# A two-layer kernel with routed experts: one address read per block, zero rows written by GpSimd, second weights' low parts made by TensorE and ScalarE

## What is computed

```python
x = x + _L0_attn_ref(_layernorm(x), W1, b1, W2, b2, W3, b3, A)   # softplus mixing
x = x + _L0_ffn_ref(_layernorm(x), Wr, Wg, Wu, Wd)               # 9 experts, top 2
x = x + _L1_attn_ref(_layernorm(x), Wk, Wq, Wv, Wu, ...)         # 16 heads, causal
x = x + _L1_ffn_ref(_layernorm(x), centroids, ...)               # 64 experts, top 8
```

## Time and profile before

| | us |
|---|---|
| median of 3 runs | 1093.57 (1092.96 to 1095.56) |
| the profiled execution, its own time | 1094.27 |
| its span in the profile | 1092.5 |
| PE busy in the span | 954.4 (87%) |
| DVE, ACT, POOL busy | 833.8, 698.2, 469.8 |
| share of the chain: PE, DVE, SyncE's queue | 59%, 12%, 10% |

### The profile page before, as it was taken

How to read it: one execution, slowest core, us unless ns; L and a number is a source line. 1 busy time by engine, 2 the same in 40 slices (tenths; PEclk the granted TensorE clock), 3 DMA queues, 4 the chain that set the end, 5 groups by cost and what they waited for, 6 DMA issues and landing times.

```text
span 1092.5 us, 20812 instructions
## 1 busy us (share of the span) xinstructions
PE 954.4 (87%) x6055; PEld 758.4 (69%) x6088; DVE 833.8 (76%) x1938; ACT 698.2 (64%) x1387; POOL 469.8 (43%) x540
## 2 busy tenths in 40 slices
PE   3573698988936999999999998999999999999998
PEld 2452687878825677767777666877777777777786
DVE  6988465666647788888888766888888878797865
ACT  3560344444424877777778765777777777777876
POOL 3578760000046565556555330444444443444343
PEclk8655799999966999999999998999999999999999
DMA  8991321111120101101101001929375655657483
GB/s 255 411 391 68 100 61 55 53 52 52 54 70 18 30 23 26 35 21 28 33 21 30 11 1 37 222 71 202 96 175 119 152 138 133 150 120 173 104 193 81
DMA packets 70164, 111.00 MB, mean 102 GB/s; under 512 B 16783, under 2 KB 55858, under 8 KB 65970
## 3 DMA queue, kind: packets, MB, share of 16 engines
q1 hardware_dynamic: 65376, 101.31, 35.4%
q0 software_dynamic: 4096, 8.40, 2.6%
q10 hardware_dynamic: 594, 0.09, 0.0%
HBM read 70.90 MB, written 38.86 MB: 100 GB/s over the span
## 4 chain that ended last, share of the span: by engine, by line
PE 59%; DVE 12%; SPq 10%; issue 7%; DMA 5%; ACT 4%; POOL 1%; DVEq 0%; POOLq 0%; ACTq 0%
SPq L536 4%; PE ps L2322 4%; PE ps L2340 4%; PE ps L2324 4%; PE ps L2323 4%; PE ps L2342 4%; PE ps L2341 4%; PE ps L2126 4%; DMA cwB<-cwd 3%; PE ps L2189 3%; PE ps L2150 3%; PE ps L2144 3%; PE ps L2172 3%; SPq L546 2%; SPq L539 2%
## 5 line engine op out<-in xcount | busy, mean ns | idle before, releaser
L880 POOL TENSOR_TENSOR hl<-h,hh 128x512 fp32r<-128x512 f32 x128 | 167.7, 1310 | 257.5 <-ACT hh L1158 257.5
L1158 ACT ACTIVATE hh<-h 128x512 fp32r<-128x512 f32 (+1 forms) x264 | 165.4, 626 | 33.1 <-DVE h L1889 30.3
L1889 DVE TENSOR_TENSOR h<-ps,cwB 128x512 f32<-128x512 f32 x192 | 130.0, 683 | 44.8 <-ACT ps L1147 32.6
L1789 DVE TENSOR_REDUCE nm<-ps 128x4 f32<-128x512 f32 (+1 forms) x128 | 116.4, 952 | 36.7 <-PE ps L2172 34.6
L778 POOL DMA_INDIRECT yg<-ys,gps x64 | 62.7, 980 | 177.5 <-issue 167.0
L1147 ACT ACTIVATE ps<-ps 128x512 f32<-128x512 f32 x192 | 111.7, 582 | 35.4 <-PE ps L2324 34.2
L2322 PE MATMUL ps<-xh,wh 128*128 128x512 f32 x256 | 103.8, 405 | 0.5 <-ACT h L1145 0.5
L1896 DVE TENSOR_TENSOR hl<-h,hh 128x512 fp32r<-128x512 f32 (+1 forms) x136 | 96.3, 708 | 10.2 <-ACT hh L1158 8.9
L2340 PE MATMUL ps<-hh,wh 128*128 128x512 f32 x256 | 102.9, 402 | 0.6 <-POOL hl L880 0.6
L2324 PE MATMUL ps<-xh,wl 128*128 128x512 f32 x256 | 100.3, 392 | 0.0
L2323 PE MATMUL ps<-xl,wh 128*128 128x512 f32 x256 | 100.3, 392 | 0.0
(11 more groups left out here) (356 smaller groups left out, 2677.9 us busy)
## 6 DMA issues: line engine op xcount, KB each, us to landing
cwB<-cwd SPq DMA_DIRECT2D x32, 1536.0 KB, 14.9
ys<-zfill SPq DMA_DIRECT2D x13, 1536.0 KB, 21.4
cwd<-cwS SPq DMA_DIRECT2D x64, 96.0 KB
xb<-xs SPq DMA_DIRECT2D x72, 64.0 KB, 1.8
ys<-yb SPq DMA_DIRECT2D x72, 64.0 KB, 1.6
x_res<-in_L_attn_x_dram SPq DMA_DIRECT2D x4, 512.0 KB, 6.6
wst<-in_L_ffn_W_up_dram SPq DMA_DIRECT2D x32, 64.0 KB, 2.1
wst<-in_L_ffn_W_down_dram SPq DMA_DIRECT2D x32, 64.0 KB, 1.9
```

The source lines that it names most:

```text
L880: pool.tensor_tensor(hl4[:, slot(u), :], h4[:, slot(u), :], hh4[:, slot(u), :].bitcast(F32), op=ALU.subtract).then_inc(u_hlp, 1)
L1158: act.activation(hh4[r, slot(u), :], h4[r, slot(u), :], ACT.Copy).then_inc(u_hh, 1)
L1789: ins = dve.tensor_reduce(nm[:, u, 4 * g:4 * g + 4], o, axis=AX.X, op=ALU.max, negate=True)
L1889: dve.tensor_tensor(h4[:, slot(u), :], first, second, op=ALU.mult).then_inc(u_h, 1)
```

## The change

- SyncE's loops are written out. A block's row is read once (`rows_at`), for the load, and the register is kept for the store.
- The nine zero stores become nine indirect scatters on GpSimd after the 64 others; `tail` now holds a row per partition. The load of block 24 still waits for them.
- Pieces 6 to 8: ScalarE makes the high parts, first in the new `HIGH_ORDER`. For the low part TensorE adds identity times `std` and negated identity times the high part in PSUM, an expert at a time (`w2_diffs`), and ScalarE copies it out (`w2_lows`): four experts in turn 4, four in turn 5, the ninth behind. The first list's bank is 2 in place of 1. `w_low(0)` moves from turn 3 to turn 4.
- Constants that only the lists need are made behind GpSimd's `zfill`, not ahead of the first wait on `consts`.
- The fills count on `c_in`, waited for ahead of the first loads; the wait for the row positions (`gp_r`) and weights stands behind block 28's load, only before the q, k, v weights are loaded.

```diff
+    FILLS = NFILL // 3 + 1
...
+        HIGH_ORDER = (6, 7, 8, 0, 1, 2, 3, 4, 5)
...
-            def rows_of(blocks, b):
-                return ds(sp_.value_load(blocks[0:1, ds(b, 1)], min_val=0, max_val=SPARE + E1 * REG - P), P)
-            def load_block(b, u, blocks):
-                sp_.dma_start(xb[:, u, :], xs[rows_of(blocks, b), :]).then_inc(xb_in[u], 16)
+                              zfill[:, :].unsqueeze(1).broadcast_to([P, 3, FILL * D])).then_inc(c_in, 16)
+            rows_at = {}
+            def load_block(b):
+                blocks = blk_a if b < NFULL else blk_b
+                rows_at[b] = sp_.value_load(blocks[0:1, b:b + 1], min_val=0, max_val=SPARE + E1 * REG - P)
+                sp_.dma_start(xb[:, b % 4, :], xs[ds(rows_at[b], P), :]).then_inc(xb_in[b % 4], 16)
             for u in range(4):
                 sp_.sem_inc(ys_out[u], 16)
-            def store_block(b, u, blocks):
+            def store_block(b):
                 sp_.wait_ge(yb_r, b + 1)
-                sp_.dma_start(ys[rows_of(blocks, b), :], yb[:, u, :]).then_inc(ys_out[u], 16)
-            def next_block(b, u, blocks):
-                sp_.wait_ge(xT_r, b + 1)
-                load_block(b + 4, u, blocks)
-                if not isinstance(b, int) or b >= 2:
-                    store_block(b - 2, (u - 2) % 4, blocks)
+                sp_.dma_start(ys[ds(rows_at.pop(b), P), :], yb[:, b % 4, :]).then_inc(ys_out[b % 4], 16)
             sp_.wait_ge(lists, 1)
             for s in range(2):
                 sp_.wait_ge(scat[s], SCATTERED)
+            sp_.wait_ge(c_in, 16 * FILLS)
             for b in range(4):
-                load_block(b, b, blk_a)
-            sp_.wait_ge(tails_in, 16 * (NFILL // 3 + 1))
-            for b in range(4):
-                next_block(b, b, blk_a)
-            sp_.wait_ge(tails, 1)
-            for e in range(E1):
-                first_row = sp_.value_load(tail[0:1, e:e + 1], min_val=0, max_val=SPARE + E1 * REG - P)
-                sp_.dma_start(xs[ds(first_row, P), :], zrow[:, :]).then_inc(tails_in, 16)
-            with sp_.Fori(1, NFULL // 4 - 1) as it:
-                for u in range(4):
-                    next_block(it * 4 + u, u, blk_a)
-            sp_.wait_ge(lists, 2)
-            sp_.wait_ge(tails_in, 16 * (NFILL // 3 + 1 + E1))
-            for s in range(2):
-                sp_.wait_ge(scat[s], SCATTERED * (NR // 2))
-            sp_.wait_ge(gp_r, 1)
-            sp_.wait_ge(w_lo, 9)
-            for u in range(4):
-                next_block(NFULL - 4 + u, u, blk_b)
-            for j, w in enumerate((WqT, WkT, WvT)):
-                sp_.dma_start(wqkv[:, j * D:(j + 1) * D], w).then_inc(c_in, 16)
-            for j, w in enumerate((qln_w, kln_w, qln_b, kln_b)):
-                sp_.dma_start(ln8[:, j, :], w.rearrange("(a n) -> a n", a=1).broadcast_to([P, S])).then_inc(c_in, 16)
-            with sp_.Fori(NFULL // 4, NBLK // 4 - 1) as it:
-                for u in range(4):
-                    next_block(it * 4 + u, u, blk_b)
-            for b in range(NBLK - 6, NBLK):
-                store_block(b, b % 4, blk_b)
+                load_block(b)
+            for b in range(NBLK):
+                if b + 4 == NFULL:
+                    sp_.wait_ge(lists, 2)
+                    sp_.wait_ge(tails_in, 16 * E1)
+                    for s in range(2):
+                        sp_.wait_ge(scat[s], SCATTERED * (NR // 2))
+                if b + 4 < NBLK:
+                    sp_.wait_ge(xT_r, b + 1)
+                    load_block(b + 4)
+                if b >= 2:
+                    store_block(b - 2)
+                if b == NFULL:
+                    sp_.wait_ge(gp_r, 1)
+                    sp_.wait_ge(w_lo, 6)
+                    sp_.wait_ge(tc1, 2 * NR + E1)
+                    for j, w in enumerate((WqT, WkT, WvT)):
+                        sp_.dma_start(wqkv[:, j * D:(j + 1) * D], w).then_inc(c_in, 16)
+                    for j, w in enumerate((qln_w, kln_w, qln_b, kln_b)):
+                        sp_.dma_start(ln8[:, j, :], w.rearrange("(a n) -> a n", a=1).broadcast_to([P, S])).then_inc(c_in, 16)
+            for b in range(NBLK - 2, NBLK):
+                store_block(b)
...
-            own.done(pool.memset(lev_w[:, :, :], 0.0))
-            own.done(pool.memset(spare[:, :], 0.0))
-            own.done(pool.memset(lcnt[:, E1:E1 + 1], float(NFULL + 1)))
-            for dst, pattern, cm, b0 in ((rev9[:, :, :], [[0, RT], [-1, E1]], 0, E1), (half_off[:, :, :], [[0, 2], [-REG, E1]], 0, -SPARE),
-                                         (base[:, :], [[REG, E1]], 0, SPARE), (w99[:, :, :], [[1, E1], [-1, E1]], 0, 0),
-                                         (prow[:, :], [[0, E1]], 1, 0), (entry[:, :], [[1, NBLK]], 0, 1)):
+            for dst, pattern, cm, b0 in ((rev9[:, :, :], [[0, RT], [-1, E1]], 0, E1), (base[:, :], [[REG, E1]], 0, SPARE),
+                                         (prow[:, :], [[0, E1]], 1, 0)):
                 own.done(pool.iota(dst, pattern=pattern, base=b0, channel_multiplier=cm,
...
-            for piece in range(6, 9):
-                src, hi, lo, arrived, n = weight_piece(piece)
-                if piece == 6:
-                    pool.wait_ge(consts, 2)
-                    pool.wait_ge(arrived, 16 * n)
-                    apart(pool, pool_passed)
-                own.link(pool.tensor_copy(hi, src))
-                own.link(pool.tensor_tensor(lo, src, hi.bitcast(F32), op=ALU.subtract))
-                pool.sem_inc(w_lo, 1)
+            pool.wait_ge(consts, 2)
...
+            pool.wait_ge(tails, 1)
+            apart(pool, pool_passed)
+            for e in range(E1):
+                pool.indirect_dma_start(out=xs, out_offset=bass.IndirectOffsetOnAxis(ap=tail[:, e:e + 1], axis=0),
+                                        in_=zrow[:, :], in_offset=None).then_inc(tails_in, 16)
             pool.wait_ge(gp_r, 1)
-            pool.wait_ge(w_lo, 9)
-            pool.wait_ge(tails_in, 16 * (NFILL // 3 + 1 + E1))
+            pool.wait_ge(w_lo, 6)
+            pool.wait_ge(tc1, 2 * NR + E1)
+            pool.wait_ge(tails_in, 16 * E1)
...
+            act.activation(negi[:, :], ident[:, :], ACT.Copy, scale=-1.0)
...
+            def w2_lows(e0, e1):
+                for e in range(e0, e1):
+                    act.wait_ge(tr1, 2 * NR + e + 1)
+                    act.activation(wd2[:, e * JC:(e + 1) * JC, 1, :], bank[e % 2][:, 0:JC * D].rearrange("p (j d) -> p j d", d=D),
+                                   ACT.Copy).then_inc(tc1, 1)
...
+                if k >= NR:
+                    w2_lows(4 * (k - NR), 4 * (k - NR) + 2)
                 if two:
                     copy_T(xmT, 6, tc2, tr2, r, 0)
                     copy_T(xmT, 6, tc2, tr2, r, 1)
                 if mix:
                     softplus(1)
+                if k >= NR:
+                    w2_lows(4 * (k - NR) + 2, 4 * (k - NR) + 4)
...
-                    if k < NR:
-                        for piece in range(3 * (k - 2), 3 * (k - 1)):
+                    if k <= NR:
+                        for piece in HIGH_ORDER[3 * (k - 2):3 * (k - 1)]:
                             w_high(piece)
             rounds(act_round)
+            w2_lows(8, E1)
...
+                dve.wait_ge(consts, 3)
...
-                    dve.tensor_copy(tail[:, :], base[:, :]).then_inc(tails, 1)
+                    dve.tensor_tensor(tail[:, :], base[:, :], prow[:, :], op=ALU.add).then_inc(tails, 1)
...
-                if 3 <= k <= NR:
-                    w_low(k - 3)
+                if k == NR:
+                    w_low(0)
+                    w_low(1)
...
+            def w2_diffs(e0, e1):
+                for e in range(e0, e1):
+                    if e == 0:
+                        pe.wait_ge(w_hi, 3)
+                    if e >= 2:
+                        pe.wait_ge(tc1, 2 * NR + e - 1)
+                    o = bank[e % 2][:, 0:JC * D]
+                    pe.matmul(o, ident[:, :], std[:, e * JC * D:(e + 1) * JC * D], start=True, stop=False)
+                    pe.matmul(o.rearrange("p (j d) -> p j d", d=D), negi[:, :], wd2[:, e * JC:(e + 1) * JC, 0, :], start=False,
+                              stop=True).then_inc(tr1, 1)
...
+                if k >= NR:
+                    w2_diffs(4 * (k - NR), 4 * (k - NR) + 2)
                 turned_second(0)
                 turned_second(1)
                 logits(0)
                 logits(1)
                 if k == NR + 1:
-                    listed(1, bank[1][0:HALF + 1, 0:NFULL])
+                    listed(1, bank[2][0:HALF + 1, 0:NFULL])
+                if k >= NR:
+                    w2_diffs(4 * (k - NR) + 2, 4 * (k - NR) + 4)
                 if k == 0:
                     turned_first(0)
                     turned_first(1)
@@ -2024,6 +2050,7 @@
                     mixed(1)
             rounds(pe_round)
+            w2_diffs(8, E1)
...
-            pe.wait_ge(consts, 3)
-            pe.wait_ge(w_hi, 6)
-            pe.wait_ge(w_lo, 9)
```

(10 more changed lines are left out.)

39 lines of the change are left out of this document (21 added, 18 removed).

## The result

| | before | after |
|---|---|---|
| median of 4 runs each | 1093.26 us | 1045.86 us (1044.41 to 1047.31) |
| profiled execution, own time / span | 1094.27 / 1092.5 | 1046.19 / 1044.5 |
| first transpose of a block | 107.87 | 100.05 |
| last yb | 307.07 | 258.14 |

The ratio is 0.9562, 95% interval 0.9543 to 0.9581: 47.4 us less. The forecast was 1042.6 us, in a range of 1039 to 1050.

The account below looks back on a forecast made before the run. SyncE's queue was taken to bound the blocks, VectorE the first stage. First-stage terms -7.7, -0.5 and +0.5, then blocks at TensorE's 2.068 us, give -51.0 us in all: span 1041.5, median 1042.6 us, range 1039 to 1050.

Parts of the forecast that it names:

- The bound: In the blocks: moves from SyncE's queue, 2.57 us a block, to TensorE, 2.068 us a block.
- SyncE's 1.86 us a block "at most": In the blocks: SyncE's time a block with one address read gone, 2.57 - 0.71 us.
- The rounds, -7.7 us: First stage: without GpSimd's weight splits the round holding them gets shorter by 7.7 us, bounds 6.4 and 8.7.
- The start, -0.5 us: Kernel start: constants moved away let the first load gate VectorE; -0.5 us, bounds 0 and -0.9.
- The ninth pair, +0.5 us: Before the first block: TensorE's ninth matmul pair and its ScalarE copy delay the first transpose 0.5 us, bounds 0 and 1.5.
- The zero rows: GpSimd: nine more scatters, 1.26 us each; block 24's load lands at 150.3, wanted at 150.7, so cost 0.
- the q, k, v weights load behind block 28's address with room as well: SyncE in the blocks: these loads fit behind block 28's address; given no cost.
- (1) block 24 late: GpSimd's scatters delay block 24's load by 5 or 8.2 us: 1047 to 1051 us; chance 0.13.
- (2) SyncE stays the bound: In the blocks: the store's cost is its issue, a block stays at 2.57 us, about 1075; chance 0.06.
- (3) a straight line that starves SyncE: In the blocks: instruction supply for the written-out code holds SyncE, over 0.95 us a block gives all back; chance 0.02.

Follow-up runs that it names:

- e2: Changed kernel, but each store on SyncE reads its block's row again, code still a straight line; 1059.42 us, ratio 0.9709.
- e3: Changed kernel, but GpSimd again makes the second weights' parts, without the extra TensorE matmuls and ScalarE copies; 1054.43 us, ratio 0.9647.
- e8: Changed kernel, q, k, v and norm loads at every third block, GpSimd's fill memset and list constants after VectorE's second xn; slower chip kind, 1099.34 us, ratio 0.9712.
- r4: Kernel before with only SyncE's loops written out and one address read a block; 1062.16 us, ratio 0.9706.
- e1: Changed kernel, but the seven q, k, v and norm loads are issued one a block, blocks 24 to 30; 1043.85 us, ratio 0.955.
- e5: Changed kernel, but the seven q, k, v and norm loads stand singly at blocks 24, 27, ... 42; slower chip kind, 1100.22 us, ratio 0.9717.
- r2: Same edits to the changed kernel as e8, on another chip of the slower kind; 1099.13 us, ratio 0.9711.
- e4: Changed kernel, but the nine zero stores are again SyncE's, behind block 7's load; 1055.52 us, ratio 0.9669.
- r3: Changed kernel with nine more GpSimd scatters behind the nine, to rows nobody reads; 1046.8 us, ratio 0.9563.
- e7: Kernel before with only SyncE's loops written out and one address read a block, on a slower kind of chip; 1102.85 us, ratio 0.9742.
- e6: Changed kernel, but four low parts of the first weights are set to zero, not subtracted; slower chip kind, 1100.91 us.

## Why the prediction was right, and where it was off

- **The bound** moved as said, from SyncE's queue to TensorE. A block takes 2.07 us (2.068 forecast) at clock 1.00. e2 shows that SyncE must be under that: at 2.29 on average the kernel loses 12.7 us by last yb.
- **SyncE's 1.86 us a block "at most"** measured 1.59. The read was 0.62 where 0.71 was taken, the loop, which the sum gave nothing, 0.25 to 0.3, and the 2.57 held a long issue (2.51 without). Since TensorE takes over at 2.07 this changed nothing in the sum.
- **The rounds, -7.7 us:** from the first x_res addition (+0.17) to the next round's stb (51.46 to 43.91, -7.55) it was 7.7 less. e3 gives the 7.5 back.
- **The start, -0.5 us,** was +0.2 in the trace of after. The forecast named what could undo it, GpSimd's memset beside the first scaling, and took half. The memset undid 0.64 of 1.18 us, which is that half, and e8 brings it out. The rest is TensorE's first matmuls, 0.72 us longer in this trace than in that of before, which differ between traces of one start by up to 1.4 us. The first addition to x_res came at 19.37 to 20.06 us, 19.85 in the mean, in the nine traces with the changed start, and at 19.85, 20.46 and 20.52 in the three with the old one. By these means the gain is 0.4 us, as forecast; one pair of traces can't tell.
- **The ninth pair, +0.5 us,** was 0: the first transpose waited for the load of its rows, 1.05 us, not for the pair. The two small errors cancel, so that the first transpose came at 100.05 for 100.2 is in part luck.
- **The zero rows:** the pitch was 1.26 us as said. Block 24's load, forecast to be issued at 146.65 and to land 3.65 us later, at 150.3, for 150.7, was issued at 144.98. With the 1.8 us that block 29's load took it would land at 146.8 (an estimate) for 150.60. So the room was nearer 4 us than the forecast's 0.4: the 3.65 us, from one load of before, was the term that was too long.
- **The step that failed** is "the q, k, v weights load behind block 28's address with room as well". It looked at GpSimd's memsets, on which these loads wait for nothing late, and not at what stands behind seven issues on SyncE: block 29's load. It costs 2.4 us. They are 4.5 us of issues against 2.1 us of room, and after that SyncE gains at most 2.07 - 1.59 = 0.48 us a block. About half of the loss hangs on one issue that took 1.68 us in place of 0.43; without it the seven are 3.2 us and the loss 1.1 (an estimate; r4, where none was long, lost 3.38 - 2.07 = 1.3). The term belonged in the sum: an issue is 0.35 us in the earlier trace rows, seven are 2.5 at the least. In e1 the gap moves and shrinks when the loads do, and in e5 and r2, which have them at every third block, it is gone.
- **The rest:** 1044.5 of span against 1041.5 is +2.0 at the last yb (+2.4 for the loads, -0.9 since the third block's hb came at 107.12 and not 108.0, the rest small steps) and +1.0 behind it, 786.4 us where before had 785.4. Traces of e1 to e4 have 784.7 to 786.7 there, so that 1 us is scatter between executions.
- **Rivals:** (1) block 24 late: not seen. (2) SyncE stays the bound: with one read it doesn't, with two (e2) it does. (3) a straight line that starves SyncE: excluded, with two reads a block went from 2.54 in the loop to 2.29 written out. The rule quoted from the Trainium skill (Runtime: NRT & Kernel Launch, Instruction fetch mechanics) has a taken branch stall only where its target isn't among the instructions already fetched. The sign agrees, 0.25 us a block less in straight code; whether that is fetching or the loop's own index and branch instructions, no run here shows.
- The range held on chips like the first. On the other kind, where before itself takes 1131 us, the gain is 27.5 us. No row of the profile of before told of that, and that the result was measured on the first kind was luck.

## What to carry to other kernels

When a queue stops being the bound, ask how much slack it now has per step, and charge it with every burst of issues that it still carries: seven issues, 4.5 us in all, met 2.1 us of room and made the one gap that could be avoided. Count a gap in TensorE's work for more than its length: behind waits of 2.1 to 8 us in e3, e4, r3 and r4 a block ran at the lower clock and took 1.5 to 1.8 us more, though not behind the 2.3 us of the kernel after. Spread a burst over the steps in portions below the slack, at every third block here and not at each. And time on more than one chip before parts are ranked: splits and zero rows together were worth about 2% on one kind and nothing that shows on the other.

## What the runs showed of the hardware

- An indirect scatter that met VectorE's four subtractions in a row (two SBUF tensors of 128x1056 each, 4.8 us together) took 5.87 to 5.95 us in place of 0.96, in twelve traces; in e7 one that began later among them took 2.03. Beside memsets of the same tiles it took 0.96 to 1.19 (e6). The Trainium skill (SBUF — State Buffer, Who interferes with whom) has a tensor_tensor leave a scatter's descriptors alone, as an inference; the measurement decides against that here.
- GpSimd's memset and constants lengthened VectorE's scaling of eight tiles by 0.7 us (3.62 against 2.96), its splits of weights by 6.4 (8.63 and 8.64 against 2.2). In r4 and e7, where the first split began 0.4 and 0.65 us ahead of the scaling and not behind its start, it took 11.60 and 11.35.
- Reading a row number into a register cost SyncE 0.62 us a block, and a loop of four blocks 0.25 to 0.3 us a block against straight code.
- Behind a gap of TensorE the clock could fall. After waits of 7.80 us (e4, block 8), 2.90 (e3) and 2.08 (r3) the granted clock was 0.50, 0.54 and 0.58 over the next block, which took 3.84, 3.70 and 3.55 us in place of 2.07. After one of 2.30 us (the kernel after, block 29) it stayed at 1.00.
- On two of the chips used, TensorE's results reached ScalarE and VectorE up to 32 us late between 57 and 163 us of the kernel, alike in six traces of five different kernels, and the kernel before was 38 us slower there. The cause is open.
